# Masked attention with layer norm: a ring of 26 groups, and subtractions and low parts issued for two groups at once

## What is computed

```python
scores = leaky_relu(x @ ks.T, slope 0.2)
scores = where(adj > 0, scores, NEG_BIG)
attn   = softmax(scores, axis=1)
out    = layernorm(x + attn @ ks)
```

## Time and profile before

| | |
|---|---|
| three runs, us | 1568.99, 1570.65, 1571.44 (median 1570.65) |
| profiled execution, us | 1569.98 |
| its span in the trace, us | 1568.1 |
| PE busy, us (share of the span) | 1511.9 (96%) |
| DVE busy | 1503.9 (96%) |
| ACT busy | 1475.3 (94%) |
| POOL busy | 1452.7 (93%) |
| chain that ended last, by engine | PE 61%, issue 13%, DVE 10%, ACT 10%, POOL 3%, DMA 2% |
| TensorE's granted clock, mean | 0.996 |
| DMA | 296 MB, mean 189 GB/s |

### The profile page before, as it was taken

How to read it: one execution, slowest core, us unless ns; L and a number is a source line. 1 busy time by engine, 2 the same in 40 slices (tenths; PEclk the granted TensorE clock), 3 DMA queues, 4 the chain that set the end, 5 groups by cost and what they waited for, 6 DMA issues and landing times.

```text
span 1568.1 us, 43439 instructions
## 1 busy us (share of the span) xinstructions
PE 1511.9 (96%) x16848; PEld 1421.2 (91%) x16848; DVE 1503.9 (96%) x1809; ACT 1475.3 (94%) x1883; POOL 1452.7 (93%) x1253
## 2 busy tenths in 40 slices
PE   5599999999999999999999999999999999999997
PEld 3389999999999999999999999999999999999996
DVE  7899999999999999999999999999999999999993
ACT  6699999999999999999999999999999999999997
POOL 4799999999999999999999999999999999999998
PEclk9999999999999999999999999999999999999999
DMA  9755666656655556655655655656556655565610
GB/s 368 245 186 182 195 194 191 196 187 193 200 190 189 199 181 197 195 189 190 193 184 193 194 191 185 195 178 196 191 186 194 191 185 191 190 194 186 196 62 8
DMA packets 107134, 296.03 MB, mean 189 GB/s; under 512 B 10801, under 2 KB 40241, under 8 KB 106929
## 3 DMA queue, kind: packets, MB, share of 16 engines
q1 hardware_dynamic: 106928, 293.25, 57.5%
HBM read 289.01 MB, written 4.19 MB: 187 GB/s over the span
## 4 chain that ended last, share of the span: by engine, by line
PE 61%; issue 13%; DVE 10%; ACT 10%; POOL 3%; DMA 2%; DVEq 0%; SPq 0%; ACTq 0%; POOLq 0%
PE weighted L771 17%; PE scores L725 9%; PE scores L727 9%; PE scores L726 9%; PE weighted L787 5%; PE weighted L783 5%; PE weighted L785 5%; ACT ring L468 4%; DVE running L631 4%; DVE ring L647 3%; ACT pt_hi L475 3%; DMA x_probe<-in_x_t 2%; DVE ring L617 2%; POOL pt_lo L376 1%; ACT scores L461 1%
## 5 line engine op out<-in xcount | busy, mean ns | idle before, releaser
L371 POOL TENSOR_TENSOR ring<-ring,floor 128x512 f32<-128x512 f32 (+2 forms) x512 | 714.5, 1396 | 43.2 <-ACT floor L488 43.1
L376 POOL TENSOR_TENSOR pt_lo<-ring,pt_hi 128x512 f16<-128x512 f32 (+1 forms) x512 | 658.9, 1287 | 22.4 <-ACT pt_hi L475 20.0
L617 DVE SCALAR_TENSOR_TENSOR ring<-adj_sb,scores 128x1024 f32<-128x1024 int32 x512 | 622.0, 1215 | 14.6 <-ACT scores L461 14.2
L461 ACT ACTIVATE scores<-scores,shrink 128x1024 f32<-128x1024 f32 x512 | 553.2, 1081 | 49.9 <-PE scores L727 46.1
L468 ACT ACTIVATE ring<-ring,lift 128x1024 f32<-128x1024 f32 x512 | 583.9, 1140 | 5.6 <-POOL ring L371 5.6
L725 PE MATMUL scores<-xt_hi,kt_hi 128*128 128x256 f16 x2048 | 560.2, 274 | 27.9 <-DVE ring L617 23.5
L727 PE MATMUL scores<-xt_hi,kt_lo 128*128 128x256 f16 x2048 | 560.5, 274 | 0.0
L726 PE MATMUL scores<-xt_lo,kt_hi 128*128 128x256 f16 x2048 | 560.2, 274 | 0.0
L631 DVE TENSOR_TENSOR running<-ring,running 128x1024 f32<-128x1024 f32 x448 | 547.3, 1222 | 0.1
L771 PE MATMUL weighted<-k_rows,ring 128*128 128x129 f32 x3584 | 488.4, 276 | 4.2 <-DVE y L668 2.9
L771 PEld LDWEIGHTS weighted<-k_rows,ring 128*128 128x128 f32 x3584 | 441.3, 192 | 16.4 <-ACT ring L468 8.7
(11 more groups left out here) (63 smaller groups left out, 473.1 us busy)
## 6 DMA issues: line engine op xcount, KB each, us to landing
adj_sb<-in_adj SPq DMA_DIRECT2D x512, 512.0 KB, 3.5
ring<-in_ks_t SPq DMA_DIRECT2D x8, 512.0 KB, 7.4
x_row<-in_x SPq DMA_DIRECT2D x32, 128.0 KB, 3.7
out<-normed SPq DMA_DIRECT2D x32, 128.0 KB, 3.6
x_probe<-in_x_t SPq DMA_DIRECT2D x29, 128.0 KB, 3.6
xt_raw<-in_x_t SPq DMA_DIRECT2D x29, 128.0 KB, 4.4
ring<-in_ks SPq DMA_DIRECT2D x12, 128.0 KB, 6.5
k_rows<-in_ks SPq DMA_DIRECT2D x12, 128.0 KB, 3.9
```

What stands on the lines that cost most here:

```text
L371: nc.gpsimd.tensor_tensor(here, here, below, ALU.subtract).then_inc(gap_ready, 1)
L376: nc.gpsimd.tensor_tensor(pt_lo[:, g % PARTS, 0:QUAD - whole, :], ring[:, g % RING, whole:, :], pt_hi[:, g % PARTS, 0:QUAD - whole, :], AL ...
L617: nc.vector.scalar_tensor_tensor(ring[:, g % RING, :, :], adj_sb[:, g % ADJS, :, :], 0.0, scores[:, g % 2, :, :], ALU.is_le, ALU.subtract)\
```

## The change

**Delays and pairs.** `RING` goes from 24 to 26 and `PARTS` from 3 to 4. `gap` on both engines and `low_part` are issued for two groups g and g + 1 (g even) as one instruction. The line of delays becomes `AT_DVE_GAP, AT_GAP, AT_EXP, AT_PART, AT_LOW, AT_WEIGH = 19, 20, 21, 22, 23, 24`, so POOL's gap of a pair stands in the slot just ahead of the pair's first exponential, and its low part one slot after the first high part.

**Tiles in parts.** `WHOLE` alternates by pairs, 2 2 1 1: of 64 tiles 24 are whole (28 before) and 40 in parts (36 before). DVE subtracts two tiles of a group, and one where g % 8 is 4 or 5; three in groups 496 and 497, and all four from group 498 on.

**Spread.** The f32 products become transposes.

**Start.** `part_rows` runs in four pieces, each behind its own piece of `high_rows`; the rows' loads have four semaphores; `high_rows` and some other steps stand a slot earlier; probes are loaded four slots ahead instead of two, at other slots; `load_x` of the first two blocks moves behind slot 20.

**End.** In the last block `turn`, `spread` and their companions stand later (`late`, `whole_late`), and its sums go to a buffer of `scores` instead of `weighted`.

The core of the diff:

```diff
-    RING = 24
+    RING = 26
+    PAIR = 2
-    WHOLE = [1 if q % 4 == 3 else 2 for q in range(GROUPS)]
+    WHOLE = [1 if q // PAIR % 2 else 2 for q in range(GROUPS)]
-    PARTS = 3
+    PARTS = 4
-    X_CUTS = (0, 3, 11, 21, BLOCKS)
+    X_CUTS = (0, 3, 8, 20, BLOCKS)
-    AT_GAP, AT_EXP, AT_PART, AT_WEIGH = 19, 21, 22, 23
+    AT_DVE_GAP, AT_GAP, AT_EXP, AT_PART, AT_LOW, AT_WEIGH = 19, 20, 21, 22, 23, 24
+    LEFT_OUT = GROUPS - 2
...
-            start, step = ((0, 0), (12, 2), (30, 12), (150, 14))[x]
+            start, step = ((0, 0), (12, 4), (34, 6), (116, 14))[x]
...
-            return 3 if g >= ALL - GROUPS else min(1 + g % 4, 2)
+            return QUAD if g >= ALL - LEFT_OUT else 3 if g >= ALL - GROUPS else 1 if g % 8 // PAIR == 2 else 2
...
# part_rows, POOL
+                for n in range(4):
+                    rows = slice(n * PARTEDS // 4, (n + 1) * PARTEDS // 4)
+                    pool.wait_ge(k_hi_ready, n + 1)
...
# gap, POOL (DVE's alike)
-                here = ring[:, g % RING, first:, :]
+                here = ring[:, g % RING:g % RING + PAIR, first:, :]
...
             def low_part(g):
-                pool.wait_ge(part_hi_ready, g + 1)
+                pool.wait_ge(part_hi_ready, g + PAIR)
...
# POOL's loop
-                g = group(s, AT_PART)
+                g = pair(s, AT_LOW)
...
-                g = group(s, AT_GAP)
-                if g is not None:
+                g = pair(s, AT_GAP)
+                if g is not None and dve_tiles(g) < QUAD:
...
             def exponentials(g):
-                act.wait_ge(gap_ready, g + 1)
-                act.wait_ge(dve_gap_ready, g + 1)
+                act.wait_ge(gap_ready, pool_gaps(g))
+                act.wait_ge(dve_gap_ready, g // PAIR + 1)
...
# spread, PE
-                    last = nc.tensor.matmul(floors[:, b % 2, j * P:(j + 1) * P],
-                                            low[:, b % 2, j:j + 1].to_broadcast([P, P]), eye[:, :],
-                                            start=True, stop=True)
+                    last = nc.tensor.transpose(floors[:, b % 2, j * P:(j + 1) * P],
+                                               low[:, b % 2, j:j + 1].to_broadcast([P, P]), eye[:, :])
```

More of the change, by code:

```diff
@@ L137, in adj_attention_layernorm @@
         k_rows_loaded = sem("k_rows_loaded")
-        ks_raw_loaded = sem("ks_raw_loaded")
+        ks_raw_loaded = [sem(f"ks_raw_loaded{n}") for n in range(4)]
         k_rows_ready = sem("k_rows_ready")
@@ L236, in probe_slot, with sums, late, pair @@
             x = x_set(b)
-            start, step = ((0, 0), (12, 2), (30, 12), (150, 14))[x]
+            start, step = ((0, 0), (12, 4), (34, 6), (116, 14))[x]
             return start + step * (b - X_CUTS[x])
+        def sums(b):
+            return weighted if b < BLOCKS - 1 else scores[:, 0, 0:2, :].rearrange("p t n -> p (t n)")
+        def late(b):
+            return 2 if b == BLOCKS - 1 else 0
+        def pair(slot, delay):
+            g = group(slot, delay)
+            return g if g is not None and g % PAIR == 0 else None
+        def pool_gaps(g):
+            return min(g // PAIR + 1, (ALL - LEFT_OUT) // PAIR)
         def least_count(g):
@@ L527, in _ @@
                         bound_x(b)
-                b = whole(s, AT_SPREAD)
+                b = whole_late(s, AT_SPREAD, 1)
                 if b is not None:
@@ L643, in gap @@
                 dve.wait_ge(floor_ready, b + 1)
-                dve.wait_ge(running_ready, least_count(g))
-                here = ring[:, g % RING, 0:tiles, :]
-                below = floors[:, b % 2:b % 2 + 1, :].to_broadcast([P, tiles, BLOCK])
+                dve.wait_ge(running_ready, least_count(g + 1))
+                here = ring[:, g % RING:g % RING + PAIR, 0:tiles, :]
+                below = floors[:, b % 2:b % 2 + 1, :].unsqueeze(1).to_broadcast([P, PAIR, tiles, BLOCK])
                 nc.vector.tensor_tensor(here, here, below, ALU.subtract).then_inc(dve_gap_ready, 1)
@@ L699, in _ @@
                     columns(g // GROUPS)
-                for early in (False, True):
-                    g = group(s, AT_GAP - 1 if early else AT_GAP)
-                    if g is not None and early == (g % GROUPS > 0):
-                        gap(g)
+                g = pair(s, AT_DVE_GAP)
+                if g is not None:
+                    gap(g)
                 g = group(s, 1)
@@ L800, in _ @@
                     magnitudes(1, bank)
-                b = whole(s, AT_TURN)
+                b = whole_late(s, AT_TURN)
                 if b is not None:
```

93 lines of the change are left out of this document (51 added, 42 removed).

## The result

The changed kernel takes **1616.01 us** (median of 4 runs, 1614.31 to 1617.69) against 1570.12 for the kernel before on the same chip: ratio 1.0292, 95% interval 1.0274 to 1.031. It is slower, as forecast, but by 46 us and not by 9; the time lies outside the range of 1544 to 1592.

What follows compares the result with a forecast made beforehand. It took the kernel as a machine in balance, TensorE issue-bound and the next engines close behind. 1569.98 + 11 (middle) - 7 (start) + 5 (end) = 1579.0, median 1579.7 us; range 1544 to 1592.

Steps and rivals of the forecast that it cites:

- the first mechanism: Middle: four times a block ACT idles 0.5 us, waiting for POOL's pair low part and gap; 47.1 us a block.
- the upper end: Middle: 47.4 us a block, with low part 3.07, gap 2.37 and handoff back 0.08.
- The rival of TensorE's pace: Middle: POOL's pairs cost 5% less than priced, blocks fall to PE's 46.05, 1545.6 us; chance 0.20.
- the walk round the block: Middle: four ACT-POOL-ACT waits of 6.37, 1.33 for the split, four ACT stretches of 4.81: 46.05, plus 1.05 for norm and floor.
- The rival of the lock: Middle: first minimum stalls 1.9 us behind POOL's instruction, 48.1 us a block, +30, 1610 us; chance 0.10.
- The probes: Middle: 14 of 26 probes lie in ACT's own stretches, 0.4 us each, adding 5.7 us.
- The start: Before the mask of group 24: POOL's subtraction in pieces -3, masks waiting less -4; -7 us (range -3 to -10).
- The end: Behind the last mask: later floor and waits, faster ACT pace, longer last low part and weighting; +5 us (range 0 to +8).
- floor and first exponential 2.3 later: End: last block's floor one slot later, POOL reaching that pair through a three-tile gap and low part; 2.3 us later.
- 1.7 us in which ACT has nothing: End: DVE's gaps from group 500 stand behind `finish` of block 30, which needs a late low part; 1.7 us.
- ACT's pace of 1.81 us a group: End: ACT's own pace from group 500 on, 1.81 us a group against 1.94 before; -2 us over 15 groups.
- the last low part and weighting +2.9: At the very end: low part covering both last groups +1.4 us, PE's two groups' parts and a whole tile +1.5.

Runs made afterwards that it cites:

- lock -0.69: Changed kernel with a linear function for the exponential; first minima read `running` in PSUM instead of a second ring slot: 1596.3 us, against 1616.38 without that edit.
- split +0.07: Changed kernel with the split of the next x block two slots earlier: 1619.08 us, ratio 1.033 to the kernel before.
- four tiles fewer: Changed kernel with 36 tiles in parts, as before the change: 1608.68 us, ratio 1.0264 to the kernel before.
- the floor on time: Changed kernel with the last block's turn, spread and floor in the same slots as every other block's: 1614.52 us, ratio 1.0294 to the kernel before.
- the two runs: Two edits of the changed kernel: last block's turn, spread and floor in the usual slots, 1614.52 us; `finish(30)` behind VectorE's gap, 1614.03 us.

## Why the prediction was wrong

**Direction and the first mechanism: right.** "Loop: 47.1 us a block, above PE's 46.05 and above today's 46.70." The pieces measured by shape in the changed kernel (count, busy us, mean ns):

```profile
L400 POOL TENSOR_TENSOR ring<-ring,floor 128x1024 f32<-128x1024 f32 x186 | 453.5, 2438 | 16.9 <-ACT floor L518 16.9
L406 POOL TENSOR_TENSOR pt_lo<-ring,pt_hi 128x1536 f16<-128x1536 f32 x128 | 398.5, 3113 | 43.7 <-ACT pt_hi L505 43.5
...
L400 POOL TENSOR_TENSOR ring<-ring,floor 128x1536 f32<-128x1536 f32 x62 | 214.3, 3457 | 0.0
```

A low part of 1,536 elements adds 3.07 net of the overlap, the upper of the two ends (3.04 taken); a gap of 1,024 not stretched by a minimum 2.33 (2.34 taken). With `mean` behind the gap blocks come 47.37 apart against 47.1 forecast and 47.4 as the upper end (its own terms add up to 47.5 there). Of the 0.27 left, the low parts are 4 x 0.03, and `deviation`, which was not priced either, may hold some. That the pairs on POOL make this path was not tried by itself: no run undoes them alone. The rival of TensorE's pace is excluded: blocks never came below 46.72 in any form of the changed kernel.

**The step that failed in the middle** is the walk round the block, "4 x 6.37 + 1.33 + 4 x 4.81": between POOL's low part and gap it puts the split, and not `mean`, which by the order of POOL's slot stands in the same place in another crossing. It was counted neither with its 0.19 us nor with its wait for VectorE's `y`. This carries the miss: the middle was forecast as 30.44 x 47.1 + 5.7 and measured as 30.44 x 48.06 + 6.0, so 29 of its 29.5 us too much lie in the block, 21 of them (0.69 a block) in this step.

**The rival of the lock** was set up as a sum: a stall of 1.9 us on VectorE's 46.2 us of work, 48.1 a block, 1610 us, chance 0.10. The number is nearly the measured one, the way to it is not. The stall is 0.96, and VectorE's work with it, 194.88 of 200 us, does not fill the block. It costs because `mean`, with the gap behind it, waits for what VectorE does ten instructions later. And the sentence that gave it its small chance, "since a stalled DVE arrives later the next time, it mostly evens out", is wrong: POOL's place in the block follows from the same loop, so the two meet at the same point in each period. The stall is there in 28 of 32 blocks, mostly some 0.95 us above the plain 1.22.

The Trainium skill, "SBUF — State Buffer", in the reading of its port diagram, states that a DVE instruction with two SBUF inputs and a GpSimd one that reads SBUF hold the port pair exclusively, and that whoever starts first keeps it for its whole instruction. The trace agrees where they meet: minimum 1.08 us behind the low part's end, and POOL's next gap, begun 0.64 us before the minimum's end, 2.86 instead of 2.36 long. By it the lock's rival deserved more than 0.10; the one meeting in the earlier trace rows that cost VectorE nothing was no evidence against it, since there VectorE had come first.

**What does not add up one by one.** Undone one by one: `mean` -0.69 a block, lock -0.69, split +0.07, four tiles fewer -0.02. Together `mean` and split give -1.23. Two loops stand side by side: ACT - high part - low part - split - gap - ACT, and VectorE - `y` - `mean` - gap - ACT - scores - mask - VectorE. By these numbers the longer one sets the pace, and shortening the other is not seen.

**The probes**, +5.7 us over clean blocks: right in size, 6.0 measured as above. In the kernel before this excess is 6.6 (1428.1 less 30.44 x 46.70), and with the new start alone 2.5 (1424.0 less the same), since the waits for probes went, 4.8 us from 86.5 to 700. What makes up the 6.0 of the changed kernel was not taken apart.

**The start**, -7, measured -3.4. The same part on the kernel before gave -5.5, so pairs and delays took back 2.1. The second first minimum of the kernel, at 63.54, was stalled by 2.0 us by a piece of the subtraction (the forecast allowed for one piece). What it had nowhere is the first exponential of all: it needs POOL's gap of a pair, 2.36 us, where one of a single group was enough. Waits in 45:83 of the changed kernel:

```profile
ACT ring L498 <- POOL ring L400: 5.6, 2, 5.1
```

With the start alone, on the kernel before, ACT waited 3.5 us at that point. That these 1.6 us are the larger part of the 2.1 was not tried by itself.

**The end**, +5, measured +9.9. In the forecast's own terms: floor and first exponential 2.3 later, measured 3.2 (15.3 against 12.1); "1.7 us in which ACT has nothing", measured 3.3 (5.54 less a plain step of 2.2); ACT's pace of 1.81 us a group, measured 1.98 from 500 to 511 (21.81 / 11) and 1.90 with the floor on time; the last low part and weighting +2.9, measured +2.9 (15.2 behind the last exponential's start, 12.3 before). The mis-sized terms are the two waits and the pace. In the pace TensorE has a part: between the exponentials of groups 500 and 511 ACT's high parts wait for its weighting three times, 1.0 us in all, and 0.2 with the floor on time. In the window 1553:1563, 1563:1573, 1573:1583, 1583:1593 and 1593:1603 of the changed kernel:

```profile
1553.00:1563.00 10.00, 6.50 (x67) 6.27 (x67) 5.45 (x6) 7.43 (x9) 9.80 (x4) 0.83 0.10 28
1563.00:1573.00 10.00, 7.09 (x72) 6.84 (x72) 4.38 (x3) 7.32 (x10) 6.47 (x3) 0.81 0.01 2
1573.00:1583.00 10.00, 9.62 (x110) 9.42 (x108) 7.92 (x10) 6.39 (x9) 4.05 (x3) 0.85 0.00 0
1583.00:1593.00 10.00, 6.67 (x67) 6.27 (x66) 6.28 (x3) 9.48 (x15) 7.69 (x6) 0.83 0.05 15
1593.00:1603.00 10.00, 9.49 (x125) 9.27 (x123) 0.00 (x0) 8.57 (x10) 5.96 (x3) 1.00 0.01 2
```

The granted clock is below 1 in four of five, while the kernel with the floor on time shows 0.83 in the first and 1.00 in the next four. How much of the end is the clock and how much the order can't be told apart, since the two runs change both.

## What to carry to other kernels

When instructions are merged, write out for each in-order queue everything that stands between the merged instruction and the one that is waited for, the tiny ones too, and ask what each of them waits for: the place of a `mean` of 0.19 us cost 16 to 17 us. Look for the second loop before costing the first, because a run that shortens the loop that does not set the pace shows nothing. A forecast of a periodic pipeline should not average over the phases at which two engines meet: here they met at one phase, in 28 of 32 periods. And of a change that bundles parts, measure the parts alone: the transposes and the start were worth 16 us, which the rest of the change had covered.

## What was unexpected of the hardware

- The stall between VectorE and GpSimd is regular: the mean of 32 first minima is 2143 ns, against 1221 of the 448 others, and of the 28 stalled ones all but the one in the start last 2.17 to 2.58 us.
- It grows when GpSimd has less idle time: in the kernel before with spread and start the first minima had a mean of 1260 ns, with two tiles more on GpSimd 1536, so a load on GpSimd took time from VectorE. With VectorE's pairs as well, which moved VectorE, it was 1745.
- GpSimd's instructions of 1,024 and 1,536 elements follow the slope of the short ones: 2.33 and 3.42 us net for a gap (2.1 ns an element), 2.10 and 3.07 for a low part in f16 (1.9 ns). The flatter slope that the earlier trace rows suggested was not found between 512 and 1,536.
- TensorE's clock fell from its upper level of 2.4 to 1.2 GHz after it had been idle for 3.5 us in the end. Products of one weighting, timeline of TensorE, changed kernel: starts 0.05 to 0.06 apart, then 0.10 to 0.11.

```profile
1558.55 0.22 PE L814 MATMUL weighted<-k_parts,pt_hi 128*128 128x129 f16 x1 [3.50 <-POOL pt_lo L406]
1558.60 0.22 PE L816 MATMUL weighted<-k_parts,pt_hi 128*128 128x128 f16 x1
...
1558.99 0.31 PE L816 MATMUL weighted<-k_parts,pt_hi 128*128 128x128 f16 x1
1559.10 0.32 PE L818 MATMUL weighted<-k_parts,pt_lo 128*128 128x129 f16 x1
```
